# Attention with cross and image tokens on one core: Q of unit 1 around K and scores of unit 0, five residuals in the stage, first output product in two pieces

## The chip, the core and the metric

The kernel runs on 1 core of a Trainium2 chip. The metric is the device time of one execution in microseconds. The engines are TensorE (PE, with its weight loads as PEld), VectorE (DVE), ScalarE (ACT), GpSimd (POOL) and SyncE (SP), which issues most DMAs.

## The reference, cut to what matters

```python
q = _split_heads(hidden_states @ w_q, HEADS)          # (2, 2048, 640), 20 heads of 32
k = _split_heads(text @ w_k, HEADS)                   # 69 text tokens of 1024
v = _split_heads(text @ w_v, HEADS)
out_text = _merge_heads(_sdpa(q, k, v))
k_ip = _split_heads(ip_h @ w_k_ip, HEADS)             # 8 image tokens, with a mask from boxes
v_ip = _split_heads(ip_h @ w_v_ip, HEADS)
out_ip = _merge_heads(_sdpa(q, k_ip, v_ip, mask=mask_ip))
out = (out_text + out_ip) @ w_out + b_out + hidden_states
```

All is float32. `_sdpa` is softmax(q k^T / sqrt(32) + mask) v. The two softmaxes over text and image tokens are separate, and their results are added.

## The kernel before, in words

The positions are cut into tiles of 512, and the 640 columns into KD = 5 groups of 128 (4 heads). A unit c is one group of one tile: 2 batches x 4 tiles x 5 groups = 40 units, with the group running fastest, so units 0 to 4 share the first tile. For each unit the kernel makes

- Q (`make_q`): 15 matmuls of 512 columns on PE. The float32 product is split: each operand has a high part and a low part (`x_hi`, `x_lo`, `wq_hi`, `wq_lo`), and the product is hi*hi, then lo weights, then lo data, 5 matmuls each. For unit 0 the order is by x tile, three kinds for each tile. ScalarE makes each high part (`high`), GpSimd each low part (`low`), VectorE those of the first tile and of w_q 0. ScalarE copies Q out of PSUM (`copy_q`).
- scores (`make_scores`): 64 small matmuls of q and k, behind `q_copied`, `k_copied`, and `scores_used` of the unit before. VectorE subtracts the maxima (`shift_text`, `shift_img`), ScalarE takes the exponential (`exp`), VectorE sums (`sums`), GpSimd normalises, VectorE transposes (`turn`), and 12 small DMAs, 8 from SP (`move`) and 4 from ScalarE (`move_rest`), regroup the result.
- O (`make_o`): 4 matmuls, two units behind. `o_high` on ScalarE and `o_low` on VectorE split it.
- the output product (`make_out`): 15 matmuls, BEHIND_OUT = 6 units behind, once all groups of a tile are there. `finish` on VectorE adds the bias and the residual, which SP loads (`residual`) and afterwards stores (`store`).

In the first units K and V are made too, a group at a time: text part (`k_text`), image part (`k_image`), a copy of it by ScalarE (`copy_k_part`), a fold into place (`k_fold`) and a copy of K (`copy_k`); V likewise with one more transpose. Their weights `wk_raw` and `wki_raw` have two slots, so `load_k(g)` waits for the fold of group g - 2.

No scheduler is at work. Each engine runs a list written by hand: `prologue()`, then `step(c)` for the 40 units, then `epilogue()`. Units 35 to 39, the last tile, get their output products in the epilogue: `make_last` accumulates them in five PSUM banks in pieces, tile by tile, as the O of units 38 and 39 become ready.

The weights w_q and w_out and the x tiles pass through the tile `stage`, with 5 slots. `JOBS` is their order, `NUMBER[job]` the place in it, and the semaphores `stage_hi` and `stage_lo` count the jobs whose high and low parts are done. A residual is loaded into one of two `res` tiles, once the store of two units earlier is done; those of the last `LATE` units go into slots of `stage`.

Of the kernel before, what the change touches and what calls it, by code (L numbers as in the profile page):

```python
# [11 lines left out]
P = 128  # L12
# [26 lines left out]
LATE = KD - 2  # L39
# [5 lines left out]
WO_JOBS = {4: (0, 1), 6: (2,), 7: (3,), 8: (4,)}  # L45
# [3 lines left out]
def xattn_kernel(nc, x, ctx, bbox, grid, eye, w_q, w_k, w_v, w_k_ip, w_v_ip, w_out, b_out, out):  # L49
# [23 lines left out]
    with es:  # L73
# [67 lines left out]
        wk_loaded = [sem(f"wk_loaded{s}") for s in range(K_SLOTS)]  # L141
        wki_loaded = [sem(f"wki_loaded{s}") for s in range(K_SLOTS)]
# [90 lines left out]
        def _(sp):  # L233
# [42 lines left out]
            def prologue():  # L276
                load(("w_q", 0))
                for kt in range(KD):
                    sp.dma_start(x0_raw[:, kt, :], x[kt]).then_inc(x0_loaded[kt], 16)  # L279
                sp.dma_start(ctx_sb[:, :, :], ctx).then_inc(ctx_loaded, 16)  # L280
                load_k(0, wki_raw, w_k_ip, wki_loaded)
                load_k(0, wk_raw, w_k, wk_loaded)
                sp.dma_start(grid_sb[:, :], grid).then_inc(grid_loaded, 16)
                sp.dma_start(box[:, :, :, :], bbox).then_inc(grid_loaded, 16)
                sp.dma_start(eye_sb[:, :], eye).then_inc(eye_loaded, 16)
                load(("w_q", 1))
                load_k(1, wk_raw, w_k, wk_loaded)
                load_k(1, wki_raw, w_k_ip, wki_loaded)
                load(("w_q", 2))
                load_k(2, wk_raw, w_k, wk_loaded)  # L290
                load_k(2, wki_raw, w_k_ip, wki_loaded)
                load(("w_q", 3))
                load_v(0, wv_raw, w_v, wv_loaded)
                load_v(0, wvi_raw, w_v_ip, wvi_loaded)
                load(("w_q", 4))
                load_v(1, wv_raw, w_v, wv_loaded)
                load_v(1, wvi_raw, w_v_ip, wvi_loaded)
                load_k(3, wk_raw, w_k, wk_loaded)
                load_k(3, wki_raw, w_k_ip, wki_loaded)
# [33 lines left out]
        def _(pool):  # L333
# [13 lines left out]
            def prologue():  # L347
                pool.wait_ge(stage_lo, 1)
                for g in range(1, 3):
                    low(("w_q", g))  # L350
# [20 lines left out]
        def _(act):  # L371
# [68 lines left out]
            def prologue():  # L440
                high(("w_q", 0))
                for kt in range(KD):
                    act.wait_ge(x0_loaded[kt], 16)
                    nc.scalar.activation(x_hi[:, 0, kt, :], x0_raw[:, kt, :], ACT.Copy).then_inc(x0_hi, 1)
                copy_q(0)
                copy_k_part(0)
                copy_k(0)
                high(("w_q", 1))
                high(("w_q", 2))
                copy_q(1)  # L450
                copy_k_part(1)
                exp(0)
                copy_k(1)
                copy_k_part(2)
                high(("w_q", 3))

            def step(c):
                if c <= KD:
# [6 lines left out]
                    if c > 0:  # L465
                        copy_vt(c - 1)
                        copy_v(c - 1)
                    exp(c + AHEAD_S)
                    copy_q(c + AHEAD_Q)
# [23 lines left out]
        def _(dve):  # L493
# [96 lines left out]

            def prologue():
                nc.vector.memset(q[:, 0, 0:P], 0.0).then_inc(zeros_set, 1)
                nc.vector.memset(prob[:, :, :, TOKENS:KEYS], 0.0)
                dve.wait_ge(stage_hi, 1)
                nc.vector.tensor_tensor(wq_lo[:, 0, :], stage[:, 0, :], wq_hi[:, 0, :].bitcast(F32),
                                        ALU.subtract).then_inc(stage_lo, 1)
                for kt in range(KD):
                    dve.wait_ge(x0_hi, kt + 1)
                    nc.vector.tensor_tensor(x_lo[:, 0, kt, :], x0_raw[:, kt, :], x_hi[:, 0, kt, :].bitcast(F32),
                                            ALU.subtract).then_inc(x0_lo, 1)  # L600
                masks()
# [28 lines left out]
        def _(pe):  # L630
# [9 lines left out]
            def make_q(c, part):  # L640
                b, t, g = place(c)
                for n in part:
                    if n == 0:
                        if c >= 1:
                            pe.wait_ge(q_copied, c)
                        if c < KD:
                            pe.wait_ge(stage_lo, NUMBER[("w_q", c)] + 1)
                        elif g == 0:
                            pe.wait_ge(stage_lo, NUMBER[("x", c + KD - 1)] + 1)
                    if c == 0 and n % 3 == 0:  # L650
                        pe.wait_ge(x0_lo, n // 3 + 1)
# [35 lines left out]
            def make_out(c):  # L687
                b, t, g = place(c)
                if g == 0:
                    pe.wait_ge(o_hi_done, c + KD)  # L690
                if c < KD:
                    pe.wait_ge(stage_lo, NUMBER[("w_out", g)] + 1)
                if out_bank(c) == Q_BANK:
                    pe.wait_ge(q_copied, UNITS)
                elif c >= 1:
                    pe.wait_ge(finished, c if out_bank(c - 1) == OUT_BANK else c - 1)
                for n in whole:
# [3 lines left out]
                last.then_inc(out_made, 1)  # L701
# [22 lines left out]
            def k_text(g, kts=range(KC)):  # L724
                pe.wait_ge(wk_loaded[g % K_SLOTS], 16 * (g // K_SLOTS + 1))
# [35 lines left out]
            def prologue():  # L761
# [61 lines left out]
            def epilogue():  # L823
# [6 lines left out]
                for g in range(3):  # L830
                    make_last(g, range(KD - 2, KD - 1))
                for g in range(3):
                    make_last(g, range(KD - 1, KD))
                for g in range(3, KD):
                    make_last(g, range(0, KD))
# [45 lines left out]
```

## Time and profile before

| | |
|---|---|
| time, median of 3 runs | 404.16 us (402.7 to 404.22) |
| time of the profiled execution | 404.16 us |
| its span | 402.3 us |
| busy: PE, DVE, POOL, ACT | 393.6, 336.9, 156.1, 129.1 us |
| granted TensorE clock, mean | 0.997 |

The span runs from the first to the last instruction; the time of the execution has 1.86 us more around it. A matmul's end is modelled, so busy time of PE is not time at its peak.

### The profile page before, as it was taken

The numbers are of one execution on the slowest core, as the hardware profiler recorded it, in microseconds if no ns is written. First come the engines' busy times: TensorE is split into PE (matmuls) and PEld (weight loads), VectorE is DVE, ScalarE is ACT, GpSimd is POOL, SyncE is SP. The second block draws the span as 40 slices with busy tenths as digits, with TensorE's granted clock in tenths as the row PEclk, the third lists the DMA queues.
The fourth block names the chain that finished last, engine by engine and source line by source line (L and its number), as shares of the span: only waits on it lengthen the run. The fifth ranks groups of instructions, "written<-read, shape, count | busy, mean of one in ns | idle before, by whom it ended". The sixth has DMA issues, their size and how long they took to land.

```text
span 402.3 us, 10795 instructions
## 1 busy us (share of the span) xinstructions
PE 393.6 (98%) x4452; PEld 292.3 (73%) x4452; DVE 336.9 (84%) x458; ACT 129.1 (32%) x196; POOL 156.1 (39%) x128
## 2 busy tenths in 40 slices
PE   8899999999999999999999999999999999999995
PEld 7688868577777776777777767777777677776773
DVE  4559779898899998998998999999989999999503
ACT  5236334453333322432323322343223322321100
POOL 0336622687326433364226442462227532222200
PEclk9999999999999999999999999999999999999998
DMA  8999736576657454764457454664466544544555
GB/s 280 382 374 333 206 78 233 158 232 171 182 158 223 132 139 138 196 190 138 137 168 231 124 148 135 209 172 145 121 211 193 142 131 127 156 124 119 178 158 182
DMA packets 42849, 72.96 MB, mean 181 GB/s; under 512 B 10544, under 2 KB 10672, under 8 KB 42800
## 3 DMA queue, kind: packets, MB, share of 16 engines
q1 hardware_dynamic: 37680, 67.02, 54.6%
q10 hardware_dynamic: 5120, 5.25, 5.2%
q8 instruction: 35, 0.57, 0.6%
q14 instruction: 14, 0.11, 0.1%
HBM read 35.53 MB, written 10.49 MB: 114 GB/s over the span
## 4 chain that ended last, share of the span: by engine, by line
PE 86%; DVE 3%; SPq 3%; DMA 3%; ACT 2%; issue 1%; ACTq 1%; DVEq 0%
PE ps L637 63%; PE ps L682 9%; PE ps L668 9%; PE ps L714 3%; SPq L259 2%; DMA wk_raw<-in_w_k 2%; ACT prob L395 1%; PE ps L720 1%; ACTq L403 1%; DVE text_max L501 1%; DVE prob L507 1%; ACT q L391 1%; DMA out_tiles<-res 1%; SPq L279 1%; DMA prob_k<-prob_t 1%
## 5 line engine op out<-in xcount | busy, mean ns | idle before, releaser
L357 POOL TENSOR_TENSOR prob<-prob,rden 128x1104 f32<-128x1104 f32 x40 | 82.2, 2056 | 200.5 <-DVE rden L530 200.5
L395 ACT ACTIVATE prob<-prob 128x1232 f32<-128x1232 f32 x40 | 50.0, 1250 | 65.7 <-DVE prob L518 65.7
L537 DVE STREAM_TRANSPOSE prob_t<-prob 128x1536 f32<-128x1536 f32 x40 | 70.7, 1767 | 0.2 <-POOL prob L359 0.2
L501 DVE TENSOR_REDUCE text_max<-ps 128x16 f32<-128x1104 f32 x40 | 52.1, 1303 | 17.1 <-PE ps L668 16.2
L637 PE MATMUL ps<-x_hi,wq_hi 128*128 128x512 f32 x200 | 59.2, 418 | 0.1
L637 PEld LDWEIGHTS ps<-x_hi,wq_hi 128*128 128x128 f32 x200 | 34.6, 188 | 33.9 <-issue 28.1
L525 DVE TENSOR_REDUCE den<-prob 128x16 f32<-128x1104 f32 x40 | 50.6, 1265 | 7.3 <-ACT prob L395 7.2
L438 ACT ACTIVATE o_hi<-ps 128x512 fp32r<-128x512 f32 x40 | 23.7, 592 | 101.9 <-PE ps L682 98.1
L637 PE MATMUL ps<-o_hi,wo_hi 128*128 128x512 f32 x200 | 55.6, 392 | 0.0
L637 PE MATMUL ps<-o_hi,wo_lo 128*128 128x512 f32 x200 | 55.1, 389 | 0.0
L637 PE MATMUL ps<-o_lo,wo_hi 128*128 128x512 f32 x200 | 55.1, 389 | 0.0
L637 PE MATMUL ps<-x_hi,wq_lo 128*128 128x512 f32 x200 | 54.4, 394 | 0.0
L637 PE MATMUL ps<-x_lo,wq_hi 128*128 128x512 f32 x200 | 52.6, 390 | 0.0
L507 DVE TENSOR_TENSOR prob<-ps,text_max 128x1104 f32<-128x1104 f32 x40 | 52.0, 1300 | 0.0
L341 POOL TENSOR_TENSOR x_lo<-stage,x_hi 128x512 fp32r<-128x512 f32 x35 | 45.1, 1314 | 2.7 <-ACT x_hi L382 2.6
L637 PEld LDWEIGHTS ps<-o_hi,wo_hi 128*128 128x128 f32 x200 | 37.4, 188 | 11.0 <-issue 3.4
L555 DVE SCALAR_TENSOR_TENSOR res<-ps,bias,res 128x512 f32<-128x512 f32 x37 | 27.3, 739 | 19.9 <-DMA res<-in_x 11.7
L682 PE MATMUL ps<-prob_k,v 77*32 77x512 f32 x320 | 43.3, 604 | 0.2
L637 PEld LDWEIGHTS ps<-x_lo,wq_hi 128*128 128x128 f32 x200 | 37.7, 189 | 7.8
L637 PEld LDWEIGHTS ps<-x_hi,wq_lo 128*128 128x128 f32 x200 | 37.6, 189 | 7.9 <-issue 0.2
L637 PEld LDWEIGHTS ps<-o_lo,wo_hi 128*128 128x128 f32 x200 | 37.5, 188 | 7.8
L637 PEld LDWEIGHTS ps<-o_hi,wo_lo 128*128 128x128 f32 x200 | 37.5, 188 | 7.8
(58 smaller groups left out, 346.4 us busy)
## 6 DMA issues: line engine op xcount, KB each, us to landing
prob_k<-prob_t SPq DMA_DIRECT2D x320, 64.0 KB
stage<-in_x SPq DMA_DIRECT2D x38, 256.0 KB, 3.0
res<-in_x SPq DMA_DIRECT2D x37, 256.0 KB
out_tiles<-res SPq DMA_DIRECT2D x37, 256.0 KB, 2.2
prob_k<-prob_t ACTq DMA_DIRECT2D x160, 32.0 KB
wki_raw<-in_w_k_ip SPq DMA_DIRECT2D x5, 512.0 KB, 7.0
wk_raw<-in_w_k SPq DMA_DIRECT2D x5, 512.0 KB, 6.7
wv_raw<-in_w_v SPq DMA_DIRECT2D x5, 512.0 KB, 8.9
```

Source lines behind the costliest of these rows:

```text
L341: nc.gpsimd.tensor_tensor(x_lo[:, b, kt, :], slot[:, 0:W], x_hi[:, b, kt, :].bitcast(F32), ALU.subtract).then_inc(stage_lo, 1)
L357: nc.gpsimd.tensor_tensor(e[:, :, 0:TEXT], e[:, :, 0:TEXT], rden[:, par, 0, :].unsqueeze(2).to_broadcast([P, QT * HG, TEXT]), ALU.mult)
L395: nc.scalar.activation(prob[:, c % 2, :, 0:TOKENS], prob[:, c % 2, :, 0:TOKENS], ACT.Exp).then_inc(exp_done, 1)
L438: nc.scalar.activation(o_hi[:, b, g, :], ps[:, O_BANK, :], ACT.Copy).then_inc(o_hi_done, 1)
L501: nc.vector.tensor_reduce(text_max[:, par, :, :], s[:, :, :, 0:TEXT], AX_X, ALU.max).then_inc(text_max_done, 1)
L507: nc.vector.tensor_tensor(e[:, :, :, 0:TEXT], s[:, :, :, 0:TEXT], text_max[:, par, :, :].unsqueeze(3).to_broadcast([P, QT, HG, TEXT]), ALU ...
L525: nc.vector.tensor_reduce(den[:, par, 0, :], e[:, :, 0:TEXT], AX_X, ALU.add)
L537: nc.vector.transpose(prob_t[:, c % 2, :, :, :].rearrange("p k n r -> p n k r"), prob[:, c % 2, :, :].rearrange("p n (k r) -> p n k r", r= ...
L555: nc.vector.scalar_tensor_tensor(out=tile, in0=ps[:, bank, :], scalar=bias[:, c % KD:c % KD + 1], in1=tile, op0=ALU.add, op1=ALU.add).then ...
L637: return nc.tensor.matmul(ps[:, bank, :], w[:, g, P * kt:P * kt + P], m[:, b, kt, :], start=(n == 0), stop=(n == 3 * KD - 1))
L668: last = nc.tensor.matmul(ps[at:at + P // 2, j, TOKENS * n:TOKENS * n + TOKENS], q[rows, c % 2, P * n + at:P * n + at + P // 2], k[rows, b ...
L682: last = nc.tensor.matmul(ps[DH * j:DH * j + DH, O_BANK, :], v[0:TOKENS, b, P * g + DH * j:P * g + DH * j + DH], p_k[:, :, :, j, :], start ...
```

## The change

- PE, prologue: Q of unit 1 is made in three pieces: matmuls 0 to 6 behind Q 0, 7 to 10 behind the fold of K 0, and 11 to 14 behind scores 0. Before, it was made in two pieces around image part 1, behind text part 1.
- SP, prologue: the load of w_q 1 moves from behind the eye matrix to ahead of ctx. The first text weights of K come in two halves with a semaphore each. The loads of K 3 go ahead of those of V 1.
- ScalarE makes the high part of w_q 1 ahead of Q 0's copy, VectorE its low part (before: GpSimd). ScalarE copies Q 1 ahead of the high part of w_q 2, and Q 2 ahead of exp 1.
- Q products of the first five units, and output products, wait for the high parts at first, and for the low parts where these are first used.
- w_out 1 is loaded and split in step 5 instead of 4. Output product 0 is made in two pieces: its first four matmuls stand ahead of scores 7, the others in the old place.
- `LATE` is 5 instead of 3, so residuals 35 and 36 also go into the stage. The last tile's products are made in groups of four and one, instead of three and two.

```diff
-LATE = KD - 2
+LATE = KD
-WO_JOBS = {4: (0, 1), 6: (2,), 7: (3,), 8: (4,)}
+WO_JOBS = {4: (0,), 5: (1,), 6: (2,), 7: (3,), 8: (4,)}
...
                 for kt in range(KD):
                     sp.dma_start(x0_raw[:, kt, :], x[kt]).then_inc(x0_loaded[kt], 16)
+                load(("w_q", 1))
                 sp.dma_start(ctx_sb[:, :, :], ctx).then_inc(ctx_loaded, 16)
                 load_k(0, wki_raw, w_k_ip, wki_loaded)
-                load_k(0, wk_raw, w_k, wk_loaded)
+                for half in range(2):
+                    kts = slice(KC // 2 * half, KC // 2 * half + KC // 2)
+                    sp.dma_start(wk_raw[:, 0, kts, :], w_k[0].rearrange("p (k n) -> p k n", n=P)[:, kts, :]).then_inc(wk0_loaded[half], 16)
...
-                load(("w_q", 1))
...
                 load(("w_q", 4))
+                load_k(3, wk_raw, w_k, wk_loaded)
+                load_k(3, wki_raw, w_k_ip, wki_loaded)
                 load_v(1, wv_raw, w_v, wv_loaded)
                 load_v(1, wvi_raw, w_v_ip, wvi_loaded)
-                load_k(3, wk_raw, w_k, wk_loaded)
-                load_k(3, wki_raw, w_k_ip, wki_loaded)
...
             def prologue():
-                pool.wait_ge(stage_lo, 1)
-                for g in range(1, 3):
-                    low(("w_q", g))
+                pool.wait_ge(stage_lo, 2)
+                low(("w_q", 2))
...
+                high(("w_q", 1))
                 copy_q(0)
                 copy_k_part(0)
                 copy_k(0)
-                high(("w_q", 1))
+                copy_q(1)
                 high(("w_q", 2))
-                copy_q(1)
...
+                    if c == 0:
+                        copy_q(c + AHEAD_Q)
                     exp(c + AHEAD_S)
-                    copy_q(c + AHEAD_Q)
+                    if c > 0:
+                        copy_q(c + AHEAD_Q)
...
                         if c < KD:
-                            pe.wait_ge(stage_lo, NUMBER[("w_q", c)] + 1)
+                            pe.wait_ge(stage_hi, NUMBER[("w_q", c)] + 1)
...
                     if c == 0 and n % 3 == 0:
+                        pe.wait_ge(x0_hi, n // 3 + 1)
+                    if c < KD and n == (1 if c == 0 else KD):
+                        pe.wait_ge(stage_lo, NUMBER[("w_q", c)] + 1)
+                    if c == 0 and n % 3 == 2:
                         pe.wait_ge(x0_lo, n // 3 + 1)
...
                 make_q(0, whole)
+                make_q(1, whole[0:7])
                 pe.wait_ge(ctx_loaded, 16)
                 k_image(0)
-                k_text(0)
+                for half in range(2):
+                    k_text(0, range(KC // 2 * half, KC // 2 * half + KC // 2))
                 k_fold(0)
+                make_q(1, whole[7:11])
                 make_scores(0)
+                make_q(1, whole[11:15])
                 k_text(1)
-                make_q(1, whole[0:6])
                 k_image(1)
-                make_q(1, whole[6:15])
...
+                elif c == BEHIND_OUT:
+                    make_out(0, whole[0:KD - 1])
+                    make_scores(c + AHEAD_S)
+                    make_o(c - 2)
+                    make_q(c + AHEAD_Q, whole)
+                    make_out(0, whole[KD - 1:])
...
-                for g in range(3):
+                for g in range(KD - 1):
                     make_last(g, range(0, KD - 2))
                 make_o(UNITS - 1)
```

The order of PE's instructions at the start, behind the third last matmul of Q 0. A row with wq_hi or wq_lo is a Q product; wki_raw is the image part of K, wk_raw the text part, eye_sb the fold, and the row with k,q the scores. Before:

```order
L637 MATMUL ps<-x_hi,wq_lo 128x512
L637 MATMUL ps<-x_lo,wq_hi 128x512
L720 MATMUL ps<-wki_raw,ctx_sb 32x128 x8
L714 MATMUL ps<-ctx_sb,wk_raw 128x2x69 x8
L738 MATMUL ps<-eye_sb,img_part 128x2x8
L668 MATMUL ps<-k,q 64x77 x32
L714 MATMUL ps<-ctx_sb,wk_raw 128x2x69 x8
L637 MATMUL ps<-x_hi,wq_hi 128x512 x5
L637 MATMUL ps<-x_hi,wq_lo 128x512
L720 MATMUL ps<-wki_raw,ctx_sb 32x128 x8
L637 MATMUL ps<-x_hi,wq_lo 128x512 x4
L637 MATMUL ps<-x_lo,wq_hi 128x512 x5
```

The same place of the changed kernel:

```order
L646 MATMUL ps<-x_lo,wq_hi 128x512
L646 MATMUL ps<-x_hi,wq_hi 128x512 x5
L646 MATMUL ps<-x_hi,wq_lo 128x512 x2
L740 MATMUL ps<-wki_raw,ctx_sb 32x128 x8
L734 MATMUL ps<-ctx_sb,wk_raw 128x2x69 x8
L761 MATMUL ps<-eye_sb,img_part 128x2x8
L646 MATMUL ps<-x_hi,wq_lo 128x512 x3
L646 MATMUL ps<-x_lo,wq_hi 128x512
L681 MATMUL ps<-k,q 64x77 x32
L646 MATMUL ps<-x_lo,wq_hi 128x512 x4
L734 MATMUL ps<-ctx_sb,wk_raw 128x2x69 x8
L740 MATMUL ps<-wki_raw,ctx_sb 32x128 x8
```

All 15 matmuls of Q 1 now stand ahead of text part 1: 7 ahead of the image part, 4 between fold and scores, 4 behind the scores.

PE around scores 7 (the row with k,q). The rows ahead of it end Q 7, the row with prob_k is the O product, and rows with wo_hi and wo_lo are output product 0. Before:

```order
L637 MATMUL ps<-x_lo,wq_hi 128x512 x5
L668 MATMUL ps<-k,q 64x77 x32
L682 MATMUL ps<-prob_k,v 32x512 x4
L637 MATMUL ps<-x_hi,wq_hi 128x512 x5
L637 MATMUL ps<-x_hi,wq_lo 128x512 x5
L637 MATMUL ps<-x_lo,wq_hi 128x512 x5
L637 MATMUL ps<-o_hi,wo_hi 128x512 x5
L637 MATMUL ps<-o_hi,wo_lo 128x512 x5
```

The same place of the changed kernel:

```order
L646 MATMUL ps<-x_lo,wq_hi 128x512 x5
L646 MATMUL ps<-o_hi,wo_hi 128x512 x4
L681 MATMUL ps<-k,q 64x77 x32
L695 MATMUL ps<-prob_k,v 32x512 x4
L646 MATMUL ps<-x_hi,wq_hi 128x512 x5
L646 MATMUL ps<-x_hi,wq_lo 128x512 x5
L646 MATMUL ps<-x_lo,wq_hi 128x512 x5
L646 MATMUL ps<-o_hi,wo_hi 128x512
L646 MATMUL ps<-o_hi,wo_lo 128x512 x5
```

Four of the five hi*hi matmuls of output product 0 moved from behind Q 8 to ahead of scores 7.

The end of SP's list; rows with in_x load a residual, rows with out_tiles store a tile. Before:

```order
L259 DMA prob_k<-prob_t 32x512 x8
L270 DMA stage<-in_x 128x512 x3
L274 DMA out_tiles<-res 128x512
L270 DMA res<-in_x 128x512
L274 DMA out_tiles<-res 128x512
L270 DMA res<-in_x 128x512
L274 DMA out_tiles<-res 128x512 x2
L274 DMA out_tiles<-stage 128x512 x3
```

And in the changed kernel:

```order
L275 DMA out_tiles<-res 128x512
L271 DMA res<-in_x 128x512
L260 DMA prob_k<-prob_t 32x512 x8
L271 DMA stage<-in_x 128x512 x5
L275 DMA out_tiles<-res 128x512 x2
L275 DMA out_tiles<-stage 128x512 x5
```

The two residual loads that stood between stores are now among five in a row ahead of all of them.

## Rows read from the trace of the kernel before

**Rows 1.** The page: busy time and share of each engine, x instructions.

```profile
PE 393.6 (98%) x4452; PEld 292.3 (73%) x4452; DVE 336.9 (84%) x458; ACT 129.1 (32%) x196; POOL 156.1 (39%) x128
```

**Rows 2.** Timeline of PE at the start: start us, us, instruction, [idle before <-releaser].

```profile
6.65 0.63 PE L637 MATMUL ps<-x_hi,wq_lo 128*128 128x512 f32 x1
...
7.08 0.43 PE L637 MATMUL ps<-x_lo,wq_hi 128*128 128x512 f32 x1
...
7.63 0.50 PE L637 MATMUL ps<-x_hi,wq_hi 128*128 128x512 f32 x1
...
10.28 0.40 PE L637 MATMUL ps<-x_lo,wq_hi 128*128 128x512 f32 x1
...
11.17 0.64 PE L720 MATMUL ps<-wki_raw,ctx_sb 128*32 128x128 f32 x16 [0.49 <-DMA wki_raw<-in_w_k_ip]
...
12.38 2.15 PE L714 MATMUL ps<-ctx_sb,wk_raw 128*128 128x138 f32 x16 [0.57 <-DMA wk_raw<-in_w_k]
...
15.14 0.94 PE L668 MATMUL ps<-k,q 32*64 32x77 f32 x64 [0.48 <-ACT k L419]
```

**Rows 3.** Timelines of PE and of ACT, steps 4 to 6.

```profile
74.60 0.40 PE L753 MATMUL ps<-eye_sb,img_part 128*128 128x16 f32 x2 [0.17 <-ACT img_part L414]
...
78.54 0.95 PE L668 MATMUL ps<-k,q 32*64 32x77 f32 x64 [0.71 <-ACT q L391]
...
83.97 1.29 PE L637 MATMUL ps<-o_hi,wo_hi 128*128 128x512 f32 x5
...
73.02 1.37 ACT L385 ACTIVATE wo_hi<-stage 128x640 fp32r<-128x640 f32 x2 [3.25 <-issue]
...
82.10 0.58 ACT L438 ACTIVATE o_hi<-ps 128x512 fp32r<-128x512 f32 x1
```

**Rows 4.** Timelines of PE and of DVE, the end.

```profile
397.08 0.39 PE L637 MATMUL ps<-o_lo,wo_hi 128*128 128x512 f32 x1
...
396.84 0.75 DVE L555 SCALAR_TENSOR_TENSOR res<-ps,bias,res 128x512 f32<-128x512 f32 x1 [3.02 <-DMA res<-in_x]
...
397.50 2.06 DVE L555 SCALAR_TENSOR_TENSOR stage<-ps,bias,stage 128x512 f32<-128x512 f32 x3
```

**Rows 5.** Windows (last: granted clock, DMA share, GB/s); two loads, issued in 4 to 5 us.

```profile
8.00:10.00 2.00, 2.00 (x10) 1.61 (x9) 1.51 (x3) 0.78 (x2) 0.00 (x0) 1.00 1.02 418
...
L246 SPq DMA_DIRECT2D wki_raw<-in_w_k_ip x1: 432/432/432, 4.0 to 4.0; - x1
...
DMA to landing us min/median/max: 7.0/7.0/7.0
...
L246 SPq DMA_DIRECT2D wk_raw<-in_w_k x1: 647/647/647, 4.5 to 4.5; - x1
...
DMA to landing us min/median/max: 7.9/7.9/7.9
```

**Rows 6.** Timeline of DVE: the later four x_lo of the first tile row.

```profile
6.88 2.63 DVE L599 TENSOR_TENSOR x_lo<-x_raw,x_hi 128x512 fp32r<-128x512 f32 x4 [0.94 <-ACT x_hi L444]
```

**Rows 7.** Timelines of PE and ACT; then the load of wk_raw issued at 24.4 us.

```profile
29.55 2.04 PE L714 MATMUL ps<-ctx_sb,wk_raw 128*128 128x138 f32 x16
...
32.23 0.95 PE L668 MATMUL ps<-k,q 32*64 32x77 f32 x64
...
43.91 2.13 PE L714 MATMUL ps<-ctx_sb,wv_raw 128*128 128x138 f32 x16
...
31.60 0.57 ACT L391 ACTIVATE q<-ps 128x512 f32<-128x512 f32 x1
...
L246 SPq DMA_DIRECT2D wk_raw<-in_w_k x1: 328/328/328, 24.4 to 24.4; - x1
...
DMA to landing us min/median/max: 5.0/5.0/5.0
```

**Rows 8.** Windows (PE, PEld, DVE, ACT, POOL busy); line 518: ns min/median/max.

```profile
200.00:300.00 100.00, 100.00 (x1133) 73.26 (x1132) 92.36 (x124) 32.17 (x45) 39.55 (x32) 1.00 0.56 164
...
L518 DVE TENSOR_TENSOR prob<-prob,img_max x40: 293/295/1366, 19.3 to 368.4; 128x128 f32<-128x128 f32 x40
```

More of the change, by code:

```diff
@@ L141, in xattn_kernel @@
         wk_loaded = [sem(f"wk_loaded{s}") for s in range(K_SLOTS)]
+        wk0_loaded = [sem(f"wk0_loaded{h}") for h in range(2)]
         wki_loaded = [sem(f"wki_loaded{s}") for s in range(K_SLOTS)]
@@ L589, in masks, with w_q_low @@
                                              NEG, None, ALU.mult))
+            def w_q_low(g):
+                dve.wait_ge(stage_hi, g + 1)
+                nc.vector.tensor_tensor(wq_lo[:, g, :], stage[:, g, :], wq_hi[:, g, :].bitcast(F32),
+                                        ALU.subtract).then_inc(stage_lo, 1)
             def prologue():
@@ L593, in prologue @@
                 nc.vector.memset(prob[:, :, :, TOKENS:KEYS], 0.0)
-                dve.wait_ge(stage_hi, 1)
-                nc.vector.tensor_tensor(wq_lo[:, 0, :], stage[:, 0, :], wq_hi[:, 0, :].bitcast(F32),
-                                        ALU.subtract).then_inc(stage_lo, 1)
+                w_q_low(0)
                 for kt in range(KD):
@@ L600, in prologue @@
                                             ALU.subtract).then_inc(x0_lo, 1)
+                w_q_low(1)
                 masks()
@@ L685, in make_o, with make_out @@
                 last.then_inc(o_made, 1)
-            def make_out(c):
+            def make_out(c, part=whole):
                 b, t, g = place(c)
[L689 to L697, printed above, removed]
+                if part[0] == 0:
+                    if c < KD:
+                        pe.wait_ge(stage_hi, NUMBER[("w_out", g)] + 1)
+                    if c == 0:
+                        pe.wait_ge(k_copied, KD)
+                        pe.wait_ge(o_hi_done, KD - 1)
+                    elif out_bank(c) == Q_BANK:
+                        pe.wait_ge(q_copied, UNITS)
+                    else:
+                        pe.wait_ge(finished, c if out_bank(c - 1) == OUT_BANK else c - 1)
+                for n in part:
+                    if g == 0 and n == KD - 1:
+                        pe.wait_ge(o_hi_done, c + KD)
+                    if c < KD and n == KD:
+                        pe.wait_ge(stage_lo, NUMBER[("w_out", g)] + 1)
                     if g == 0 and n >= 2 * KD:
@@ L700, in make_out @@
                     last = product(out_bank(c), wo_hi, wo_lo, o_hi, o_lo, b, g, n)
-                last.then_inc(out_made, 1)
+                    if n == 3 * KD - 1:
+                        last.then_inc(out_made, 1)
             def make_last(g, kts):
@@ L724, in k_text @@
             def k_text(g, kts=range(KC)):
-                pe.wait_ge(wk_loaded[g % K_SLOTS], 16 * (g // K_SLOTS + 1))
+                if g == 0:
+                    pe.wait_ge(wk0_loaded[kts[0] * 2 // KC], 16)
+                else:
+                    pe.wait_ge(wk_loaded[g % K_SLOTS], 16 * ((g + 1) // K_SLOTS))
                 if g >= 2:
@@ L826, in epilogue @@
                 pe.wait_ge(scores_used, UNITS)
-                for g in range(3):
+                for g in range(KD - 1):
                     make_last(g, range(0, KD - 2))
                 make_o(UNITS - 1)
-                for g in range(3):
+                for g in range(KD - 1):
                     make_last(g, range(KD - 2, KD - 1))
-                for g in range(3):
+                for g in range(KD - 1):
                     make_last(g, range(KD - 1, KD))
-                for g in range(3, KD):
-                    make_last(g, range(0, KD))
+                make_last(KD - 1, range(0, KD))
             turns(prologue, step, epilogue)
```

## The prediction

> **What bounds the kernel now.** I read the page first, for the busy shares. TensorE (PE) works 393.6 us of a span of 402.3, and VectorE comes next with 336.9 [rows 1]. The change neither adds nor removes matmul work, so the time can only fall where PE stands still, and after its last matmul. The timeline of PE shows, in brackets, where it stands: 0.49 us until the first image weights of K land, 0.57 for the text weights, 0.48 for ScalarE's copy of K [rows 2]; further on 0.17 for an image part and 0.71 for the copy of Q [rows 3]. Behind a Q product these values are too small by a constant: such a matmul is drawn 0.39 or 0.40 us long, while the next starts about 0.23 after it, so PE is free some 0.16 us before the drawn end. Lastly the tail: the last matmul starts at 397.08 and is drawn to 397.47, and the span ends at 402.3, 4.8 us in which PE has nothing left [rows 4].
>
> **The start: Q of unit 1 around K and scores of unit 0.** PE issues the last matmul of Q 0 at 10.28, is free at 10.51 and starts the image part at 11.17, the text part at 12.38 and the scores at 15.14, each behind a wait [rows 2]: 0.49 + 0.16 + 0.57 + 0.48 = 1.70 us of standing still. The change puts 7 matmuls of Q 1 (7 x 0.23 = 1.6 us) ahead of the image part and 4 (0.9 us) after the fold. PE then reaches the image part at 12.0, 0.8 us later than now, and the scores of unit 0 some 0.6 us later than 15.14, with 7 + 4 matmuls already done that used to stand behind text part 1. What must be there in time:
>
> - The load of w_q 1 now stands ahead of ctx and both K loads. It has 327,680 bytes, and the DMA moves 418 GB/s in 8 to 10 us [rows 5], so all behind it lands about 0.8 us later. The image weights landed at 4.0 + 7.0 = 11.0 and now land at 11.8, just ahead of PE at 12.0. The text weights landed at 4.5 + 7.9 = 12.4 [rows 5], now 13.2, but their first half of 262,144 bytes 0.63 us sooner, at 12.5. PE wants the halves at about 12.6 and 13.6. I leave 0.1 us of waiting here.
> - The x tiles are not moved. VectorE has its last x_lo at 6.88 + 2.63 = 9.51 [rows 6]; The low part of w_q 1 comes next there; at 2.63 us for four tiles of 512 columns [rows 6] I take 0.9 for its 640, so it is there at about 10.5. PE wants it with the sixth matmul of Q 1, at about 11.6.
> - A Q matmul may now start on the high parts. In Q 0 the fourth started at 7.63, behind x_lo of tile 1 (from 6.88, when x_hi was ready). The third started at 7.08, and the second at 6.65, 0.43 before it: 512 columns at the lower level of 1.2 GHz [rows 2, 6]. So the fourth starts at 7.51 now: 0.12 us, or 0.45 if the pace has risen by then. I take 0.12.
>
> Sum of the start: 1.70 + 0.12 - 0.10 = 1.7 us. Both ends: 0.9 if PE is held for the whole 0.8 us of the later loads, 2.1 at the faster pace.
>
> **What could give it back.** Scores of unit 2 start at 32.23, right behind ScalarE's copy of Q 2 (31.60, 0.57 long) [rows 7], which stands behind exp of unit 1, and so behind VectorE. With the old order the gain would stick there. The change copies Q 2 first, as soon as its last matmul is done, and this gives about 0.1 us on top. On SP, load_k(3) now stands ahead of load_v(1). Its text weights landed at 24.4 + 5.0 = 29.4 and were used at 29.55 [rows 7]: no slack, and PE will want them at 27.8. The load waits for the second fold, itself 1.7 us earlier (22.7), and the 1 MB of load_v(1) no longer goes first, which is 2.5 us at the rate above. So they land near 27. Without the swap this place would cost up to 1.7 us. The V weights behind it have time: they land at about 30, and the second text part of V runs at 43.91 [rows 7]. Queued behind the waiting load on SP are also the x tiles, K 4, V 2 and the moves of unit 0, which start up to 1 us later against PE's order; the O product that needs these moves comes after that text part of V.
>
> **The first output product.** One load, one high and one low of w_out leave step 4 for step 5. ScalarE made both highs at 73.02 (1.37 us) ahead of the image part copy; with one, the copy comes 0.7 us sooner and PE's wait at 74.60, 0.17 + 0.16 = 0.33 us, goes [rows 3]. Then four matmuls of output 0 (0.91 us) fill the gap ahead of the scores of unit 7. PE stood 0.71 + 0.16 = 0.87 us there and started them at 78.54; now it starts them about 0.09 later with 0.91 done: 0.8 us. The high of w_out 1 (half of 1.37 us) now goes ahead of the copy of o of unit 4, which stood at 82.10, 0.58 long; it ends at 83.4, and PE wants it with the fifth matmul of output 0, whose product stood at 83.97 [rows 3]. It fits with 0.6 us to spare; if it doesn't, it costs what is missing.
>
> **The tail.** VectorE finishes tile 36 at 396.84, after 3.02 us of waiting for a residual, and three more tiles from 397.50 for 2.06 us, so the last ends at 399.56 [rows 4]. With five residuals in the stage, tiles 35 to 38 are finished while PE works on the last one; the last finish starts at 397.50 and ends 0.75 us later, at 398.25: 1.31 us. The five loads in a row delay store 33 by two issues, about 1 us, and nothing waits for it. Four groups of partial products instead of three ahead of O of unit 39 only give its moves more time.
>
> **Sum.** 1.7 + 0.1 + 0.33 + 0.8 + 1.31 = 4.2 us. The profiled execution took 404.16 us, which is also the median of the three runs; 402.3 of it is the span and 1.86 lies around it. The time is 404.16 - 4.2 = **399.9 us**, a span of 398.1.
>
> **Rivals.** (a) The start is bound by the DMA. For it: the DMA's share is 1.02 in 8 to 10 us [rows 5], PE already waits for two landings, and rows of 2 KB may move slower than rows of 4. If the loads land another 1 us late, the start gives 0.7 or less: 401.0 us. (b) The order on PE is no longer the bound after 30 us: ScalarE or VectorE holds it, since VectorE's work for unit 0 starts 0.6 us later than now, and most of what start and first product give is lost. Left are the tail and a third of the rest: 1.3 + 1.0 = 2.3, so 401.9; with the tail alone 402.9, which can't be told from no change. Against it: VectorE idles 7.64 of the 100 us from 200 to 300 [rows 8], and can catch up. (c) Slower, by one mechanism: VectorE against GpSimd. The subtraction of the image maximum takes 293 ns, 295 in the median of 40 and 1366 at worst [rows 8]. VectorE's slack is 7.64 us in 100, 0.68 in a step of 8.9. If the new phase put this subtraction beside GpSimd's normalisation in every step, a step would take 1.07 - 0.68 = 0.39 more, over some 33 steps 12.9, less the 4.2: 412.9 us. It outweighs the gains from 11 such steps on, and shows as slower from 16. Against it: the phase within a step comes from the same waits as before, and the median is the short one.
>
> The Trainium skill (SBUF — State Buffer, Who interferes with whom) says that a VectorE instruction with two SBUF inputs and a GpSimd instruction that reads SBUF exclude each other for the whole instruction. By that rule the long cases are such meetings, and a shift in phase could multiply them; the trace agrees as far as 1366 against 293 ns goes.
>
> (d) Nothing that can be told: the removed waits are short, and the three runs of before differ by 1.5 us. It is the far end of (b).
>
> **How the numbers follow.** Chances: the sum as worked out 0.60, (a) 0.18, (b) with (d) 0.18, (c) 0.03, another failure 0.01. The sum's own range is 399.2 to 401.0: a start of 0.9 to 2.1 and a first product of 0.7 to 1.1, not both at one end. The range to hold 8 in 10 takes in (a) and most of (b): 398.8 to 402.2. A difference under 0.5%, 2 us, is what a measurement of this kernel can't tell from none. Faster by more: 0.60 + 0.17 + 0.09 = 0.86; same 0.10; slower 0.04.
>
> **What would show it.** Right: no wait of PE over 0.2 us before 16 us; scores 0 near 15.8, scores 2 near 30.4; no wait for the copy of Q near 75 us; the last finish alone, right behind the last matmul, which starts near 394.2. Wrong: waits for wki_raw or wk_raw over 0.5 us, a new wait at text part 3 or at the fifth matmul of output 0, the last three finishes still in a row, or VectorE without idle time in the steady steps.

## The result and the profile after

The changed kernel takes 400.7 us in the median of 19 runs (399.36 to 403.67), the kernel before 404.16 (402.62 to 405.69). The ratio is 0.9923, with a 95% interval of 0.9904 to 0.9942: about 3.1 us less, 2.3 to 3.9 (the two medians as they stand differ by 3.5). I had forecast 399.9 us, 4.2 less, and a range of 398.8 to 402.2. So direction and range were right, and the gain was a quarter smaller than forecast. The profile of the changed kernel shows that its inside was not what I had worked out.

The profiled execution was the second longest of the 19, 403.38 us with a span of 401.6. So the waits below need not be those of an ordinary execution, and the size of the gain has to come from the timed runs. The waits of PE in it, in total, times and longest:

```profile
PE ps L734 <- DMA wk_raw<-in_w_k: 1.4, 1, 1.4
PE ps L787 <- DVE q L602: 1.1, 1, 1.1
PE ps L776 <- ACT img_part L416: 1.0, 1, 1.0
PE ps L646 <- ACT q L393: 0.7, 1, 0.7
PE ps L646 <- ACT x_hi L446: 0.6, 1, 0.6
PE ps L646 <- ACT o_hi L440: 0.6, 1, 0.6
```

The waits of [rows 2, 3] are gone: the image and text weights of K 0, the copy of K, the copy of Q ahead of scores 7. In their place stand four that I had not forecast or had ruled out: Q 1 for the copy of Q 0, text part 3 for its weights, the fold of V 1 for ScalarE's copy of an image part, and the fifth matmul of output 0 for the copy of o. The wait for `x_hi` lies in Q 0, and the one for DVE, ahead of the first matmuls of all, is there in the kernel before too. PE's timeline shows where they are:

```profile
10.22 0.39 PE L646 MATMUL ps<-x_lo,wq_hi 128*128 128x512 f32 x1
11.29 1.43 PE L646 MATMUL ps<-x_hi,wq_hi 128*128 128x512 f32 x5 [0.69 <-ACT q L393]
...
13.10 0.64 PE L740 MATMUL ps<-wki_raw,ctx_sb 128*32 128x128 f32 x16
13.68 2.15 PE L734 MATMUL ps<-ctx_sb,wk_raw 128*128 128x138 f32 x16
...
16.91 0.95 PE L681 MATMUL ps<-k,q 32*64 32x77 f32 x64
...
30.38 2.15 PE L734 MATMUL ps<-ctx_sb,wk_raw 128*128 128x138 f32 x16 [1.43 <-DMA wk_raw<-in_w_k]
...
49.63 0.39 PE L776 MATMUL ps<-eye_sb,img_part 128*128 128x16 f32 x2 [0.99 <-ACT img_part L416]
...
85.92 0.50 PE L646 MATMUL ps<-o_hi,wo_hi 128*128 128x512 f32 x1 [0.57 <-ACT o_hi L440]
...
397.90 0.39 PE L646 MATMUL ps<-o_lo,wo_hi 128*128 128x512 f32 x1
```

The last matmul starts at 397.90, 0.8 us later than in [rows 4]. In this execution PE gained nothing at all; what is left is the tail. VectorE's timeline at the end:

```profile
392.88 2.79 DVE L560 SCALAR_TENSOR_TENSOR stage<-ps,bias,stage 128x512 f32<-128x512 f32 x4 [2.28 <-PE ps L646]
398.32 0.75 DVE L560 SCALAR_TENSOR_TENSOR stage<-ps,bias,stage 128x512 f32<-128x512 f32 x1 [2.65 <-PE ps L646]
```

The first four finishes (x4) are done early and the last stands alone, 0.03 us behind the drawn end of the last matmul. From the start of the last matmul to the end of the span it is 401.6 - 397.90 = 3.7 us, where it was 5.2 [rows 4].

### The profile page after: what moved, and what is told of

Read it like the earlier page. It is cut to its first block, busy times and chain, and to the rows that moved or that the text cites. A ratio compares the mean times of both kernels' runs of the same rounds, so it can differ in the third digit from the quotient of the medians.

```text
span 401.6 us, 10790 instructions
## 1 busy us (share of the span) xinstructions
PE 392.8 (98%) x4452; PEld 291.1 (72%) x4452; DVE 339.1 (84%) x459; ACT 129.7 (32%) x196; POOL 154.2 (38%) x127
## 4 chain that ended last, share of the span: by engine, by line
PE 85%; DMA 5%; DVE 4%; POOL 2%; ACT 1%; SPq 1%; issue 1%; DVEq 0%
PE ps L646 66%; PE ps L695 9%; PE ps L681 8%; DMA stage<-in_x 3%; PE ps L734 2%; DMA x_raw<-in_x 1%; DMA stage<-in_w_out 1%; POOL prob L359 1%; SPq L242 1%; DVE den L530 1%; ACT prob L397 1%; DVE text_max L506 1%; DVE prob L512 1%; DVE prob L523 1%; DVE prob_t L542 0%
## 5 line engine op out<-in xcount | busy, mean ns | idle before, releaser
L681 PEld LDWEIGHTS ps<-k,q 32*64 32x64 f32 x2560 | 32.3, 130 | 13.0 <-issue 12.2
```

The costliest lines, as they stand in the source:

```text
L681: last = nc.tensor.matmul(ps[at:at + P // 2, j, TOKENS * n:TOKENS * n + TOKENS], q[rows, c % 2, P * n + at:P * n + at + P // 2], k[rows, b ...
```

## The experiments

Twelve kernels were run, in three groups of four, and the kernel before was timed again with each group. All ratios are to that kernel. The two numbers in brackets behind a ratio are its 95% interval. In microseconds 0.1% is 0.4 us. Each kernel has one profile, of one of its executions. Edits are to the changed kernel, except in the first three, which take one part of the change into the kernel before.

### The three parts alone

**The tail.**

```diff
-LATE = KD - 2
+LATE = KD
...
-                for g in range(3):
+                for g in range(KD - 1):
                     make_last(g, range(0, KD - 2))
                 make_o(UNITS - 1)
```

> The kernel before with nothing but the tail of the change: five residuals in the stage, last products in groups of four and one. By the prediction's term for the tail it gains 1.3 us, and the last finish stands alone behind the last matmul. If the tail had been paid for by waits elsewhere (stores or moves held up behind five loads in a row), it would gain 0.5 us or less.

Measured: 402.22 us against 404.14, ratio 0.9956 [0.9941, 0.9971], so 1.8 us less (1.2 to 2.4). The finish stands alone (397.59, last matmul at 397.17, span 400.8: 3.6 us instead of 5.2). The term was 1.3; the profile gives 1.6. The rest over 1.3 lies behind the last finish: before, 2.7 us passed from its end at 399.56 to the end of the span, here 2.5.

**The first output product.**

```diff
-WO_JOBS = {4: (0, 1), 6: (2,), 7: (3,), 8: (4,)}
+WO_JOBS = {4: (0,), 5: (1,), 6: (2,), 7: (3,), 8: (4,)}
...
+                elif c == BEHIND_OUT:
+                    make_out(0, whole[0:KD - 1])
+                    make_scores(c + AHEAD_S)
+                    make_o(c - 2)
+                    make_q(c + AHEAD_Q, whole)
+                    make_out(0, whole[KD - 1:])
```

> The kernel before with nothing but the first output product in two pieces and w_out 1 a step later. By the prediction's terms it gains 0.33 + 0.8 = 1.1 us. By the trace of the changed kernel, where w_out 1 landed late and PE waited 0.57 us for the copy of o of unit 4, it gains about 0.5 us.

Measured: 403.62 us, ratio 0.9992 [0.9973, 1.0011]: 0.3 us less, between 1.1 less and 0.4 more. In its profile PE goes from scores 6 (71.24) to scores 8 (87.08) in 15.84 us, where the kernel before takes 16.54 (70.92 to 87.46): 0.7 us of the forecast 1.1. The interval holds both a gain of 0.7 and none.

**The start.** The whole change of the prologue and of the Q products, without the other two parts.

> The kernel before with nothing but the start of the change (Q of unit 1 in three pieces, the loads in their new order, halves of the first text weights). By the prediction it gains 1.7 + 0.1 = 1.8 us. By my theory from the trace of the changed kernel (Q of unit 1 waits for its PSUM bank, the first fold comes later, the DMA runs dry between 15 and 18 us and text part 3 waits) it gains 1 us or less, and has a wait of over 1 us at text part 3.

Measured: 403.71 us, ratio 0.9998 [0.9976, 1.0019]. The start alone gives nothing that can be told; the other theory's "1 us or less" holds, and text part 3 waits 1.2 us. Text part 3 starts at 29.56 (before: 29.55) and scores 3 at 42.68 (before: 42.78), so in this profile the wait at text part 3 takes the whole gain of the start. The timeline of PE also shows something that neither theory had: the fold of V 1 waits on top, and scores 4 come at 54.55 (before: 54.34).

```profile
48.33 0.40 PE L769 MATMUL ps<-eye_sb,img_part 128*128 128x16 f32 x2 [0.69 <-ACT img_part L416]
```

### One cause at a time

**The bank.** `make_q(1)` waits for `q_copied`, since Q 0 and Q 1 are made in the same PSUM bank. I had read past this wait.

```diff
+        def q_bank(c):
+            return WARM_BANK if c == 0 else Q_BANK
...
-                        if c >= 1:
+                        if c >= 2:
                             pe.wait_ge(q_copied, c)
```

> The changed kernel, with Q of unit 0 made in PSUM bank 3, so that Q of unit 1 need not wait for ScalarE's copy of Q of unit 0. By my theory the wait of 0.7 us ahead of Q 1 goes, the first fold comes 0.7 us earlier, the DMA is dry for less long, and the time falls by 0.7 to 1.4 us against the changed kernel. By the rival (the start is bound by the landing of K's weights) the wait only moves to the image and text parts, and the time falls by 0.2 us or less.

Measured: 401.32 us, ratio 0.9937 [0.9915, 0.9960], no better than the changed kernel's 0.9923. The wait for Q's copy is gone, the image part waits only 0.24 us for its weights, and text part 3 doesn't wait (28.26). So the forecast of the start nearly comes true up to there, and PE is at scores 3 at 41.40, 1.4 us ahead of the kernel before. Then it waits 1.3 us at the fold of V 1, which starts at 47.63; before it started at 47.58. Of the 1.4 us nothing is left at the fold, and 0.5 at scores 4 (53.87 against 54.34). That text part 3 doesn't wait here need not come from the bank, as the next experiment shows.

**The dry stretch of the DMA.** The load of K 2 waits for the first fold, and everything behind it on SP with it. The windows of the changed kernel (last column GB/s, ahead of it the DMA's share and TensorE's granted clock):

```profile
15.00:16.00 1.00, 1.00 (x11) 1.00 (x10) 0.93 (x5) 0.01 (x1) 0.00 (x0) 1.00 0.71 284
16.00:17.00 1.00, 1.00 (x12) 0.55 (x17) 0.27 (x2) 0.29 (x1) 0.00 (x0) 1.00 0.27 57
17.00:18.00 1.00, 1.00 (x65) 0.91 (x66) 0.03 (x1) 0.00 (x0) 0.00 (x0) 1.00 0.67 143
24.00:26.00 2.00, 2.00 (x78) 1.68 (x70) 1.97 (x4) 1.20 (x3) 0.64 (x1) 1.00 0.91 251
```

Before, the first three had 379, 258 and 361. The fold had moved from 14.37 to 15.66, and 0.5 MB that could have flowed in these 3 us did not. The experiment loads what waits for nothing first:

```diff
-                load_k(2, wk_raw, w_k, wk_loaded)
-                load_k(2, wki_raw, w_k_ip, wki_loaded)
                 load(("w_q", 3))
                 load_v(0, wv_raw, w_v, wv_loaded)
+                load_k(2, wk_raw, w_k, wk_loaded)
+                load_k(2, wki_raw, w_k_ip, wki_loaded)
```

> The changed kernel, with w_q 3 and the first V text weights (0.85 MB that wait for nothing) loaded ahead of K 2, which waits for the first fold. By my theory the DMA no longer runs dry between 15 and 18 us, text part 3 has its weights 1 us or more earlier, and the time falls by 1 us or more against the changed kernel. By the rival (what is late at text part 3 is only the wait for the second fold) the landing moves by less than 0.3 us and the time stays.

Measured: 400.96 us, ratio 0.9925 [0.9895, 0.9955]: no gain over the changed kernel. Both halves of the mechanism are seen, 401, 427 and 417 GB/s in the three windows and text part 3 without a wait at 28.75. The second half is weaker than it looks. Three later kernels have the changed kernel's order of loads up to this place (w_out 1 first, the tiles' highs later, V 2 later), and text part 3 doesn't wait in them either (29.30, 27.99, 27.96), although the DMA is as dry in the first of them, from 16 to 18 us:

```profile
16.00:17.00 1.00, 1.00 (x8) 0.91 (x8) 0.70 (x4) 0.30 (x1) 0.00 (x0) 1.00 0.22 87
17.00:18.00 1.00, 1.00 (x53) 0.64 (x58) 0.00 (x0) 0.00 (x0) 0.00 (x0) 1.00 0.47 57
```

From its issue to its landing the text weight load of K 3 took 6.7 us in the changed kernel's profile and 3.9 to 6.4 in the six others with that order, but 3.7 to 3.8 in the three with K 2 behind the free loads. So the new order helps this load, and the wait of 1.4 us is not in every execution of the changed kernel; what decides it is not shown.

In this experiment the gain again ends at the fold of V 1, now with 2.1 us of waiting, and something comes on top:

```profile
47.00:48.00 1.00, 0.00 (x0) 0.00 (x0) 1.00 (x1) 0.51 (x2) 0.57 (x1) 1.00 1.08 254
48.00:49.00 1.00, 0.12 (x1) 0.12 (x2) 0.07 (x1) 0.83 (x3) 1.00 (x2) 0.99 0.53 137
49.00:50.00 1.00, 1.00 (x4) 0.90 (x5) 0.00 (x0) 0.30 (x1) 0.92 (x1) 0.50 0.25 86
50.00:51.00 1.00, 1.00 (x4) 0.81 (x3) 0.00 (x0) 0.00 (x0) 0.00 (x0) 0.50 0.17 61
51.00:52.00 1.00, 1.00 (x5) 0.72 (x5) 0.00 (x0) 0.00 (x0) 0.00 (x0) 0.50 0.07 25
52.00:53.00 1.00, 1.00 (x5) 0.81 (x5) 0.00 (x0) 0.80 (x2) 0.00 (x0) 0.80 0.02 6
```

The third number from the end is the granted clock. After PE had done nothing from 47 to 48.88, it is 0.50, the level of 1.2 GHz, for over 3 us. From the fold of V 1 to V's text part 2 (the next matmuls with wv_raw) it took 54.64 - 48.88 = 5.8 us, where the changed kernel took 53.80 - 49.63 = 4.2: the wait cost 1.6 us a second time. The Trainium skill (TensorE: Matmul & The Clock Gate, HAM oscillation) says that waits between bursts of matmuls put PE back to half clock. Its example waits for DMAs, and for longer; the rows here agree in kind, with a wait of 2.1 us for a copy of ScalarE.

**The swap of K 3 and V 1.**

```diff
-                load_k(3, wk_raw, w_k, wk_loaded)
-                load_k(3, wki_raw, w_k_ip, wki_loaded)
                 load_v(1, wv_raw, w_v, wv_loaded)
                 load_v(1, wvi_raw, w_v_ip, wvi_loaded)
+                load_k(3, wk_raw, w_k, wk_loaded)
+                load_k(3, wki_raw, w_k_ip, wki_loaded)
```

> The changed kernel, with the loads of V 1 ahead of those of K 3 again. By the prediction the swap is worth up to 1.7 us: text part 3 then waits about 1.5 us longer. If the DMA is behind anyway, V 1's load fills time in which K 3's can't start, and the time changes by less than 0.5 us.

Measured: 401.79 us, ratio 0.9936 [0.9914, 0.9958], the same as the changed kernel within the interval. Text part 3 waits 1.2 us and starts at 30.23, where the changed kernel waited 1.4 and started at 30.38. By this pair my 1.7 us for the step were wrong: with V 1 ahead the DMA moves 420 GB/s in 24 to 26 us instead of 251. But the pair is of single profiles. The load of K 3 took 6.4 us to land here, and 3.9 to 6.7 in the seven profiles with the changed kernel's order. So the swap is worth nothing that the time shows, and its worth at text part 3 stays open.

**w_out 1 ahead of the x tiles.**

```diff
-            return [("x", first + k) for k in X_JOBS.get(c % KD, ()) if exists(first + k)] + jobs
+            xs = [("x", first + k) for k in X_JOBS.get(c % KD, ()) if exists(first + k)]
+            return jobs + xs if c == KD else xs + jobs
```

> The changed kernel, with w_out 1 ahead of the three x tiles of step 5 in loads and splits. By my reading of the trace the wait of 0.57 us for the copy of o of unit 4 goes, and the time falls by about 0.5 us. If the order on PE isn't the bound there, the time stays and the wait comes back somewhere within the next steps.

Measured: 400.07 us, ratio 0.9890 [0.9864, 0.9917]. What held the copy of o is seen in ScalarE's timeline of the changed kernel:

```profile
84.65 0.74 ACT L387 ACTIVATE wo_hi<-stage 128x640 fp32r<-128x640 f32 x1 [1.16 <-DMA stage<-in_w_out]
85.29 0.58 ACT L440 ACTIVATE o_hi<-ps 128x512 fp32r<-128x512 f32 x1
```

I had counted the instruction of w_out 1's high, 0.7 us, but not its load, which SP issues fourth in a row, at 80.0, and which landed 4.6 us later. Placed first, its high is done at 81.6, and the copy of o starts at 83.05, before PE wants it. From scores 6 to scores 8 it is 15.6 us (70.97 to 86.53), 1.0 less than before and 0.6 less than in the changed kernel (72.47 to 88.66, 16.2): the forecast 1.1, nearly. The ratio is lower than the changed kernel's by 0.33%, with intervals that overlap. And the order is not the whole cause. The copy of o still stands behind the highs of three x tiles, and in the next experiment, with w_out 1 first as well, the last of these tiles is late and PE waits 0.4 us:

```profile
84.63 0.63 ACT L389 ACTIVATE x_hi<-stage 128x512 fp32r<-128x512 f32 x1 [0.65 <-DMA stage<-in_x]
85.17 0.58 ACT L445 ACTIVATE o_hi<-ps 128x512 fp32r<-128x512 f32 x1
```

Of the seven profiles with the changed kernel's order in step 5, PE waits there in four (0.57, 0.45, 0.18 and 0.17 us) and not in the other three (bank, V 1 ahead, V 2 later).

**The three corrections together** (bank, DMA order, w_out 1).

> The changed kernel with three corrections together: Q of unit 0 in bank 3, w_q 3 and V text weights ahead of K 2, w_out 1 ahead of the x tiles. If the three causes are the whole difference to the prediction and don't overlap, it reaches the changed kernel's time less 2 to 3 us, near 398 us, 1.5 per cent below the kernel before. If the landing of K's weights binds the start it gains 1 us or less.

Measured: 400.64 us, ratio 0.9910 [0.9880, 0.9941], so 0.5 us under the changed kernel by the ratios and not 2 to 3. The profile shows one text part at 21.17 after 0.7 us of waiting for its weights, the next of K at 28.61 without a wait, and then the fold of V 1 at 48.14, after 1.6 us, with the granted clock at 0.50 again from 50 to 52.

### The fold of V 1

Ten kernels had put PE at scores 3 up to 2.3 us apart, and all had the fold of V 1 between 47.6 and 49.6. The four kernels of this section are the last four rows:

| | scores 3 | fold of V 1 | its wait | scores 4 |
|---|---|---|---|---|
| before | 42.78 | 47.58 | - | 54.34 |
| changed | 43.69 | 49.63 | 1.0 | 55.88 |
| tail alone | 42.65 | 48.10 | 0.5 | 54.32 |
| first product alone | 43.15 | 48.45 | 0.4 | 54.68 |
| start alone | 42.68 | 48.33 | 0.7 | 54.55 |
| bank | 41.40 | 47.63 | 1.3 | 53.87 |
| DMA order | 41.84 | 48.88 | 2.1 | 56.72 |
| V 1 ahead of K 3 | 43.35 | 48.31 | - | 54.53 |
| w_out 1 first | 42.35 | 48.15 | 0.7 | 54.41 |
| three corrections | 41.61 | 48.14 | 1.6 | 55.98 |
| tiles' highs later | 41.04 | 45.84 | - | 51.96 |
| V 2 later | 41.03 | 45.95 | - | 52.18 |
| bank, w_out 1, highs | 41.71 | 46.50 | - | 52.62 |
| the same, loads too | 41.50 | 46.30 | - | 52.42 |

In the kernel before, ScalarE has its copy done at 47.2, 0.4 us ahead of the fold. The two highs ahead of it start when ScalarE has issued its own four DMAs ("issue"), not when the tiles land:

```profile
45.72 1.15 ACT L382 ACTIVATE x_hi<-stage 128x512 fp32r<-128x512 f32 x2 [2.52 <-issue]
46.77 0.28 ACT L419 ACTIVATE k<-ps 128x154 f32<-128x154 f32 x1
46.95 0.27 ACT L414 ACTIVATE img_part<-ps 128x128 f32<-128x128 f32 x1
```

With the tail alone these four DMAs took 3.7 us instead of 2.7 to issue, and that is its wait of 0.5. ScalarE's timeline of the changed kernel says what holds it there. It waits for x tiles 8 and 9, takes their highs, and only then comes to the copy for the fold of V 1:

```profile
47.18 0.63 ACT L384 ACTIVATE x_hi<-stage 128x512 fp32r<-128x512 f32 x1 [3.08 <-DMA stage<-in_x]
48.60 0.63 ACT L384 ACTIVATE x_hi<-stage 128x512 fp32r<-128x512 f32 x1 [0.79 <-DMA stage<-in_x]
49.13 0.28 ACT L421 ACTIVATE k<-ps 128x154 f32<-128x154 f32 x1
49.31 0.27 ACT L416 ACTIVATE img_part<-ps 128x128 f32<-128x128 f32 x1
```

The two loads were issued at 36.4 and 37.8. The first landed by 47.2, when ScalarE goes on, and the second 10.8 us after its issue; in the kernel before they took 4.7. They stand behind 2 MB of K 4 and V 2, whose last part landed at 43.5 instead of 39.6. The bytes that weren't moved in the two dry stretches fit this; that they are the cause isn't shown.

Two experiments take this apart from opposite ends.

```diff
                     if c == 2:
                         o_high(c - 2)
+                        for job in step_jobs(1):
+                            high(job)
...
                 move_rest(c)
-                for job in step_jobs(c):
+                for job in (step_jobs(c) if c != 1 else []):
                     high(job)
```

> The changed kernel, with ScalarE's highs of x tiles 8 and 9 moved from the end of step 1 to the end of step 2, behind the copies of V 1, so that the fold of V 1 no longer stands behind the landing of these tiles. My theory after eight runs: in every one of them, wherever PE stood before, this fold came at 47.6 to 49.6 us, because ScalarE's queue was held there by tiles that land near 46 to 48 us; what the start gains is given back at this place. Then the fold comes near 48.1 less the wait, the wait of 0.7 to 2.1 us goes, and the time falls by 1 us or more against the changed kernel. Rival: the start itself gives nothing more, and the time stays within 0.5 us.

Measured: 400.58 us, ratio 0.9912 [0.9887, 0.9937]. The wait is gone, and the fold starts at 45.84. In the time the gain is 0.4 us by the ratios, less than the 1 us I expected, and not resolved from the changed kernel.

```diff
                 if c == 0:
                     load_k(4, wk_raw, w_k, wk_loaded)
                     load_k(4, wki_raw, w_k_ip, wki_loaded)
-                    load_v(2, wv_raw, w_v, wv_loaded)
-                    load_v(2, wvi_raw, w_v_ip, wvi_loaded)
...
+                if c == 1:
+                    load_v(2, wv_raw, w_v, wv_loaded)
+                    load_v(2, wvi_raw, w_v_ip, wvi_loaded)
```

> The changed kernel, with the 1 MB of V 2 loaded behind x tiles 8 and 9 instead of ahead of them. The same theory by the other end: the tiles land 2.5 us or more earlier, near 44 to 45 us, ScalarE isn't held, the wait ahead of the fold of V 1 falls below 0.3 us and the time falls by 0.7 to 1.5 us. Rival: the lateness is that of ScalarE's own DMA issues, and both the wait and the time stay.

Measured: 399.55 us, ratio 0.9890 [0.9865, 0.9915], 1.3 us under the changed kernel by the ratios, with intervals that overlap. Of PE's waits only two are left:

```profile
PE ps L788 <- DVE q L603: 1.1, 1, 1.1
PE ps L647 <- ACT q L394: 0.7, 1, 0.7
```

The second tile is there at 43.5, ScalarE takes their highs when its own DMA issues are done, and PE doesn't stop:

```profile
44.40 1.16 ACT L385 ACTIVATE x_hi<-stage 128x512 fp32r<-128x512 f32 x2 [2.96 <-issue]
45.45 0.28 ACT L422 ACTIVATE k<-ps 128x154 f32<-128x154 f32 x1
45.63 0.27 ACT L417 ACTIVATE img_part<-ps 128x128 f32<-128x128 f32 x1
```

Scores 4 start at 52.18, 2.2 us ahead of the kernel before, and the last matmul at 393.14, where I had forecast 394.2.

Not all of these 2.2 us come from the edit: 1.6 are there at text part 3 (27.96 against 29.55), ahead of the first load that it moves, since PE didn't wait there in this execution. What the edits can have done lies between scores 3 and scores 4. With PE early at scores 3 (41.0 to 41.8) this stretch takes 10.9 to 11.2 us in the four kernels of this section, and 12.5, 14.4 and 14.9 with the bank, the three corrections and the DMA order (before: 11.6). That is the evidence that an early PE loses its lead at this fold, and that it need not.

**Bank, w_out 1 first and the highs later**, and then **the same with the loads in an order without the first dry stretch**.

> The changed kernel with Q of unit 0 in bank 3, w_out 1 ahead of the x tiles of step 5, and the highs of x tiles 8 and 9 behind the copies of V 1. If the gains of the start were given back at the fold of V 1, the bank's 0.7 us now shows in the time: 2 to 3 us below the changed kernel, near 398 us. If they were lost elsewhere, it is at 400 us as the corrections were without the move.

> The kernel of the run before this one, with the loads in an order in which none that waits for nothing stands behind one that waits for a fold: w_q 3 and the V 0 text weights ahead of K 2, the V 1 text weights ahead of K 3, the V 2 image weights behind x tiles 8 and 9. If the dry stretches of the DMA still cost PE time, it gains another 0.5 to 1 us; if the moved highs have made them harmless, it equals the run before within 0.3 us.

Measured: 399.35 us, ratio 0.9880 [0.9854, 0.9907], and 399.60 us, ratio 0.9892 [0.9868, 0.9916]. The first has the lowest ratio of all, 1.2% under the kernel before and 1.7 us under the changed kernel by the ratios (the two intervals just touch), a little less than the 2 to 3 I expected; in its profile an O product waits 1.0 us for its moves at 54.54. The second can't be told from it, although its DMA moves over 410 GB/s all through 15 to 18 us: once ScalarE isn't held by the tiles, this dry stretch costs nothing that can be told.

## Why the prediction was right, and where it was not

**Range, direction and main number.** 400.7 lies in the range, and the gain was 3.1 of 4.2 us. The largest part of it was the tail, which I had put second, and the start, which I had put first, gave nothing that can be told alone. That the number held is in part luck: the parts as measured alone add up to 2.2 us, or 402.0, which is just inside the range.

**The start (term 1.7 us).** This step failed. The start alone measured 0.1 us, with an interval from 1.0 less to 0.8 more. Three things were wrong in it. First, I placed Q 1 directly behind Q 0 and did not count the wait on `q_copied` in `make_q`. PE waits 0.7 us for it in each of the seven profiles in which Q 0 and Q 1 share the bank, and in the changed kernel's the image part started at 13.10 and not at 12.0, the scores at 16.91 and not near 15.8. Secondly, a later first fold (15.66 instead of 14.37) holds SP's queue and leaves the DMA dry; I had checked whether the weights arrive for PE, not whether SP's next load could be issued. In the profiles of the changed kernel and of the start alone, PE then waits 1.4 and 1.2 us at text part 3, and there the gain ends. Thirdly, where PE does come early to scores 3, it loses most or all of its lead at the fold of V 1. Rival (b) had this form, "most of what start and first product give is lost", with ScalarE named; its own time, 401.9, was too pessimistic, in part since the tail gave more. I had gone through the waits of the kernel before for who comes late once PE is early, but only to text part 3 and scores 2; ScalarE's queue near 46 us had no wait in PE's list, because it was just in time. The last four kernels show the third cause: with the tiles early, or their highs late, PE keeps its lead past the fold. None of the three, removed alone, changed the time by an amount that is clear of the intervals; how the missing 1.6 us divide among them stays open.

**Q of unit 0 on high parts (0.12 us).** Not settled. In the profile after, PE waits 0.59 us for `x_hi`, behind a late x tile, and that hides it. The last matmul of Q 0 starts between 9.78 and 10.43 in the three profiles with the old order, and between 9.31 and 10.71 in the eleven with the new one.

**Scores 2 (0.1 us).** The wait for the copy of Q 2 is gone, as said.

**The swap of K 3 and V 1.** The step said that without it up to 1.7 us would be lost, and that K 3 would land near 27. It landed at 30.4 in the changed kernel's profile and at 26.8 with the highs later. Undoing the swap moved text part 3 by 0.15 us against the former; against the latter nothing was tried.

**The first output product (0.33 + 0.8 us).** The mechanism held and the size was off: 0.7 alone and 0.35 in the changed kernel, between scores 6 and 8. The missing part is the wait at the fifth matmul, 0.57 us, which I had said would fit "with 0.6 us to spare". The load of w_out 1 was left out; with it first the stretch gives 1.0 in three profiles and 0.6 in that of the three corrections, where an x tile was late, and in the seven profiles with the changed kernel's order 0.3 to 1.2.

**The tail (1.31 us).** The mechanism held, and the gain was larger: 1.6 in the profile, 1.8 in the time (1.2 to 2.4).

**The DMA-bound start (a) and VectorE against GpSimd (c).** The image weights were to land at 11.8. They landed at 12.3 in the changed kernel, and between 11.6 and 12.8 in the other profiles with this start. With the bank free PE waited 0.2 to 0.3 us for them, so (a) was a small loss, hidden by the bank. (c) was not seen: the subtraction of the image maximum took 21.7 us in 40 instead of 19.7, with a median of 295 ns as before, and no profile after has a wait of PE for VectorE in the steady steps.

What stays open: the parts alone add up to 2.2 us, the whole gave 3.1, and the intervals allow both. The profiled execution of the changed kernel was 0.7% above its median, and which of its four waits the ordinary ones have can't be read from one profile.

## What to carry to other kernels

When work is moved so that the leading engine comes early, follow each helper's queue forward to the point where it is just in time, not only the waits that the profile lists: a queue without a wait can be without slack too, and then the load or copy at its head takes the gain back. One profile shows the waits of one execution; before a wait is given a cause, look whether kernels that leave that cause alone have it too. For a load behind a slot, ask two things, when its data lands and what its issuer holds back meanwhile. For a product moved up behind another of its kind, look at the bank first.

## What was unexpected of the hardware

An idle time of PE can cost twice: after the waits of 2.1 and 1.6 us at the fold of V 1 (DMA order, and the three corrections together) the granted clock fell to 0.50, and in both the stretch from there to V's text part 2 took 5.8 us instead of 4.2; after the waits of 1.0 and 1.3 us at the same place (changed, bank) it stayed at 1.00. And the landing time of one 256 KB load, issued at the same place of the program, went from 4.7 to 10.8 us; with the 1 MB of V 2 behind it instead of ahead it was 6.9.
